# Gated cross-attention on one core: product and residual kept in the context's PSUM bank, memory loaded a step earlier, GpSimd's subtractions cut into pieces

## What is computed

```
memory_proj = memory @ W_mem.T                                # 375 x 512
attn  = softmax(x @ memory_proj.T / sqrt(512))
context = attn @ memory_proj
gate  = sigmoid(concat(x, context) @ W_gate.T + b_gate)
fused = x + gate * context
out   = fused * rsqrt(mean(fused^2) + 1e-6) * norm_w
```

## Time and profile before

| what | value |
|---|---|
| median of three runs | 345.56 us |
| profiled execution | 344.57 us |
| its span, first to last instruction | 342.8 us |
| mean granted TensorE clock | 0.935 |
| TensorE matmul busy | 295.7 us (86%) |
| VectorE busy | 210.1 us (61%) |
| ScalarE busy | 173.7 us (51%) |
| GpSimd busy | 173.3 us (51%) |

### The profile page before, as it was taken

One profiled execution on the slowest core, in us unless ns is written; L12 is line 12 of the kernel. 1 busy time (PEld: TensorE's weight loads), 2 busy tenths in 40 slices (PEclk: granted clock), 3 DMA queues, 4 the chain that ended last, 5 costly groups with the idle time before them and its releaser, 6 DMA issues. The chain is left out here.

```text
span 342.8 us, 4761 instructions
## 1 busy us (share of the span) xinstructions
PE 295.7 (86%) x1479; PEld 246.7 (72%) x1479; DVE 210.1 (61%) x356; ACT 173.7 (51%) x363; POOL 173.3 (51%) x135
## 2 busy tenths in 40 slices
PE   8998588899897799999897699999998599957791
PEld 5977477778786598788686598787687488846561
DVE  4994535856867526855876536757876635555644
ACT  5862535546636436454556446544655445425531
POOL 1342445834848544744857643745857732443502
PEclk9999699999999599999999589999999689998997
DMA  7957744867764573866855573775846563652421
GB/s 293 408 149 237 232 112 122 262 185 231 213 180 125 139 224 117 264 188 185 246 148 135 154 242 115 229 224 147 254 115 179 167 183 113 175 157 71 118 64 62
DMA packets 52872, 61.40 MB, mean 179 GB/s; under 512 B 38640, under 2 KB 38896, under 8 KB 52592
## 3 DMA queue, kind: packets, MB, share of 16 engines
q1 hardware_dynamic: 52848, 61.10, 59.4%
HBM read 43.25 MB, written 7.34 MB: 148 GB/s over the span
## 5 line engine op out<-in xcount | busy, mean ns | idle before, releaser
L886 POOL TENSOR_TENSOR memT_lo<-mems_raw,memT_hi 128x752 fp32r<-128x752 f32 x21 | 38.1, 1815 | 58.8 <-ACT memT_hi L540 58.8
L736 DVE STREAM_TRANSPOSE blocks_am<-am 128x256 f32<-128x256 f32 x32 | 14.2, 445 | 70.5 <-ACT am L588 70.5
L886 POOL TENSOR_TENSOR mem_lo<-mems_raw,mem_hi 128x768 fp32r<-128x768 f32 x22 | 48.1, 2188 | 10.6 <-ACT mem_hi L540 10.5
L904 POOL TENSOR_TENSOR guarded<-meansq,eps 128x1 f32<-128x1 f32 x27 | 5.5, 203 | 78.3 <-ACT work L597 78.2
L573 ACT ACTIVATE probs<-score_ps,shift 112x375 f32<-112x375 f32 x32 | 18.3, 573 | 46.8 <-DVE shift L716 46.8
L766 DVE SCALAR_TENSOR_TENSOR work<-work,rstd,norm_w 128x512 f32<-128x512 f32 (+1 forms) x29 | 38.6, 1334 | 1.1 <-POOL rstd L939 1.0
L602 ACT ACTIVATE work<-work 128x512 f32<-128x512 f32 (+1 forms) x29 | 17.8, 618 | 40.2 <-DVE work L745 40.2
L540 ACT ACTIVATE memT_hi<-mems_raw 128x752 fp32r<-128x752 f32 x22 | 18.3, 831 | 34.6 <-DMA mems_raw<-in_mems 34.5
L758 DVE SCALAR_TENSOR_TENSOR work<-work,x_rows 128x512 f32<-128x512 f32 (+1 forms) x29 | 34.4, 1189 | 0.3
L350 PE MATMUL gate_ps<-wgx_hi,xT_hi 128*128 128x512 f32 x108 | 33.2, 433 | 0.1
L352 PE MATMUL gate_ps<-wgx_lo,xT_hi 128*128 128x512 f32 x108 | 31.8, 419 | 0.0
(11 more groups left out here) (128 smaller groups left out, 719.0 us busy)
## 6 DMA issues: line engine op xcount, KB each, us to landing
mems_raw<-in_mems SPq DMA_DIRECT2D x20, 760.0 KB, 5.1
x_rows<-in_x SPq DMA_DIRECT2D x28, 256.0 KB, 5.3
out<-work SPq DMA_DIRECT2D x27, 256.0 KB, 5.5
first_raw<-in_mems SPq DMA_DIRECT2D x9, 760.0 KB, 4.8
pT_raw<-blocks_p SPq DMA_DIRECT2D x128, 48.0 KB, 2.6
xT_raw<-in_xT SPq DMA_DIRECT2D x7, 640.0 KB, 6.0
amT_raw<-blocks_am SPq DMA_DIRECT2D x128, 32.0 KB, 1.9
xT_raw<-in_xT SPq DMA_DIRECT2D x3, 512.0 KB, 6.0
```

The costliest lines, as they stand in the source:

```text
L736: dve.transpose(turned_am, am_blocks).then_inc(blocks_am_ready, 1)
L886: return pool.tensor_tensor(out, in_, high.bitcast(F32), ALU.subtract)
L904: pool.tensor_tensor(guarded[:, s], meansq[:, s], eps[:], ALU.add).then_inc(guarded_ready, 1)
```

## The change

- SyncE loads the memory of batch s+3 in step s where it loaded that of batch s+2; `load_mems(5)` is added to the opening. It now waits for the low parts of batch s itself, made in the same step.
- `gate_context` writes its product over the context in `ctx_ps`; `fuse` adds x there, in place; `square` (ScalarE) and `norm` (VectorE) read that bank. The SBUF tiles u and h go. `context(t)` therefore waits for `y_ready`, the norm of the tile before. The last tile's two halves use the two `q_ps` banks.
- ScalarE does `pT_high(s-1)` ahead of `exponentials(s)`, and `square` ahead of `amT_high`.
- VectorE does `norm(before)` ahead of `turn_am(s-1)` where it stood behind it.
- GpSimd's subtractions are one instruction per chunk: 2 for memT, 3 for mem, 4 for x.

```diff
-        work = sb("work", [P, 7, D])
-        z, h, y, u = work[:, 0:2], work[:, 2:4], work[:, 4:6], work[:, 6]
+        work = sb("work", [P, 6, D])
+        z, y = work[:, 0:2], work[:, 4:6]
...
-        late_ps = [ctx_ps, gate_ps[1]]
+        late_ps = q_ps
...
             load_mems(4)
+            load_mems(5)
...
-                if s + 2 < BATCHES:
-                    load_mems(s + 2)
+                if s + RAW < BATCHES:
+                    load_mems(s + RAW)
...
             def context(t, cols=ALL, bank=ctx_ps):
                 pe.wait_ge(wmT_lo_ready, EC)
-                if t > 0:
-                    pe.wait_ge(u_ready, t)
+                if bank is ctx_ps and t > 0:
+                    pe.wait_ge(y_ready, t)
...
-            def square(t, cols=ALL, i=0):
+            def square(t, cols=ALL, i=0, bank=ctx_ps):
...
-                act.activation(z[:, t % 2, cols], h[:, t % 2, cols], ACT.Square, scale=D ** -0.5,
+                act.activation(z[:, t % 2, cols], bank[:, cols], ACT.Square, scale=D ** -0.5,
...
+                if s - 1 < BATCHES:
+                    pT_high(s - 1)
                 for n in softmaxes_at(s)[:1]:
                     exponentials(n)
-                if s - 1 < BATCHES:
-                    pT_high(s - 1)
+                if before is not None:
+                    square(before)
                 if s - 2 < BATCHES:
                     amT_high(s - 2)
-                if before is not None:
-                    square(before)
...
-                dve.scalar_tensor_tensor(out=u[:, cols], in0=z[:, t % 2, cols], scalar=1.0, in1=bank[:, cols],
+                dve.scalar_tensor_tensor(out=bank[:, cols], in0=z[:, t % 2, cols], scalar=1.0, in1=bank[:, cols],
...
-                dve.scalar_tensor_tensor(out=h[:, t % 2, cols], in0=u[:, cols], scalar=0.5,
+                dve.scalar_tensor_tensor(out=bank[:, cols], in0=bank[:, cols], scalar=0.5,
                                          in1=x_rows[:, t % X_SLOTS, cols],
...
-                dve.scalar_tensor_tensor(out=y[:, t % 2, cols], in0=h[:, t % 2, cols],
+                dve.scalar_tensor_tensor(out=y[:, t % 2, cols], in0=bank[:, cols],
...
                     amT_low(s - 2)
+                if before is not None and before < LAST - 1:
+                    norm(before)
                 if s - 1 < BATCHES:
                     turn_am(s - 1)
                 for n in softmaxes_at(s)[1:]:
                     maximum(n)
-                if before is not None and before < LAST - 1:
-                    norm(before)
...
             def split_xT(g, unit):
                 c, n = UNITS[unit]
                 pool.wait_ge(xT_hi_ready, N_UNITS * g + unit + 1)
-                low(xT_lo[:, :, c:c + n], raw_of(unit), xT_hi[:, :, c:c + n]).then_inc(xT_lo_ready, 1)
+                for i in range(DC):
+                    piece = low(xT_lo[:, i, c:c + n], raw_of(unit)[:, i], xT_hi[:, i, c:c + n])
+                piece.then_inc(xT_lo_ready, 1)
...
-                low(memT_lo[:, n % 2], memT_raws[n % RAW], memT_hi[:, n % 2]).then_inc(memT_lo_ready, 1)
+                for c in range(EC):
+                    piece = low(memT_lo[:, n % 2, c], memT_raws[n % RAW][:, c], memT_hi[:, n % 2, c])
+                piece.then_inc(memT_lo_ready, 1)
...
-                low(mem_lo[:, n % 2], mem_raws[n % RAW], mem_hi[:, n % 2]).then_inc(mem_lo_ready, 1)
+                for c in range(KC):
+                    piece = low(mem_lo[:, n % 2, c], mem_raws[n % RAW][:, c], mem_hi[:, n % 2, c])
+                piece.then_inc(mem_lo_ready, 1)
```

More of the change, by code:

```diff
@@ L696, in _ @@
             for i, cols in enumerate(HALVES):
-                square(LAST, cols, i)
+                square(LAST, cols, i, late_ps[i])
         @block.vector
@@ L750, in gate_context, with fuse, norm @@
                 dve.wait_ge(ctx_done, t + 1 + i)
-                dve.scalar_tensor_tensor(out=u[:, cols], in0=z[:, t % 2, cols], scalar=1.0, in1=bank[:, cols],
+                dve.scalar_tensor_tensor(out=bank[:, cols], in0=z[:, t % 2, cols], scalar=1.0, in1=bank[:, cols],
                                          op0=ALU.add, op1=ALU.mult).then_inc(u_ready, 1)
-            def fuse(t, cols=ALL, i=0):
+            def fuse(t, cols=ALL, i=0, bank=ctx_ps):
                 dve.wait_ge(x_loaded[t % X_SLOTS], 16 * (t // X_SLOTS + 1))
                 dve.wait_ge(u_ready, t + 1 + i)
-                dve.scalar_tensor_tensor(out=h[:, t % 2, cols], in0=u[:, cols], scalar=0.5,
+                dve.scalar_tensor_tensor(out=bank[:, cols], in0=bank[:, cols], scalar=0.5,
                                          in1=x_rows[:, t % X_SLOTS, cols],
                                          op0=ALU.mult, op1=ALU.add).then_inc(h_ready, 1)
-            def norm(t, cols=ALL):
+            def norm(t, cols=ALL, bank=ctx_ps):
                 dve.wait_ge(rstd_ready, t + 1)
@@ L876, in _ @@
             for i, cols in enumerate(HALVES):
-                fuse(LAST, cols, i)
+                fuse(LAST, cols, i, late_ps[i])
             norm(LAST - 1)
-            for cols in HALVES:
-                norm(LAST, cols)
+            for i, cols in enumerate(HALVES):
+                norm(LAST, cols, late_ps[i])
         @block.gpsimd
```

## The result

| | before | after |
|---|---|---|
| median | 345.61 us (4 runs, 343.83 to 346.28) | 318.74 us (4 runs, 317.85 to 321.14) |
| ratio | 1 | 0.9241 [0.9178, 0.9304] |
| span of the profiled execution | 342.8 us | 316.4 us |
| mean granted clock | 0.935 | 0.956 |

The kernel became 26.9 us faster where 19.4 were forecast. The time lies within the range (317 to 337) but outside the band of the forecast itself (320 to 330), and the reasons don't all hold, as the experiments show.

The account below looks back on a forecast made before the run. The prediction took TensorE's own work plus its holes to bound the kernel. Terms -5.0 - 1.7 - 4.5 - 1.0 - 7.2 = -19.4 us from 344.57 gave 325.2, stated as 325.5; range 317 to 337 us.

Parts of the forecast that it names:

- The memory a step earlier: Memory load a step earlier: nearly all of ScalarE's 34.5 us DMA wait goes, but the term is only -1.7 us.
- Residual and norm in PSUM: VectorE's residual and norm take 0.69 us each, returning 34 us to VectorE; shorter TensorE waits for pT_low give -5.0 us.
- Steps 10, 18, 26: Steps without a tile: next score starts earlier, 1.5 us in each of three, -4.5 us.
- the clock: After the thin stretch in steps without a tile, the clock drops again but shorter: -1.0 us, bounds 0 and -7.
- the clock stays up: Rival: no clock drops at steps 10, 18, 26, giving 318 us; chance 0.08.
- Step 30: With the memory already there, score(30) to attend(30) takes 10.6 us instead of 16.5; whole term -7.2 us.
- Wrong if the exponential waits for pT: Sign against the forecast: ScalarE's exponential is held up by pT; no size given.
- The hole only changes its name: Rival: only the DMA wait goes, everything else is bounded elsewhere, such as late pT; gain 11 us, 334 us; chance 0.12.
- Context's wait for the norm: Context now waits for the previous tile's norm; 0.8 us of slack in the shortest steps, priced at 0.
- GpSimd's pieces: 122 extra GpSimd pieces at 0.15 us, 18 us, hidden except where counted.
- SyncE's wait for mem_lo: SyncE waits for mem_lo(s) before loading; GpSimd ends it about when SyncE used to reach that load, priced at nothing.

Follow-up runs that it names:

- a2: Changed kernel with product and residual in SBUF tiles again, orders kept, context waiting for `u_ready`: 321.01 us, 0.9374 of the kernel before.
- b2: Kernel before with the PSUM part alone, the norm still behind `turn_am`: 344.12 us, 1.0032 of the kernel before.
- b3: Kernel before with the earlier load of the memory alone: 319.26 us, 0.9306 of the kernel before.
- b1: Changed kernel with ScalarE's old order, exponential ahead of `pT_high` and `amT_high` ahead of `square`: 317.35 us, 0.9241 of the kernel before.
- a1: Changed kernel with the memory load back at its old place (batch s+2): 344.69 us, 1.0059 of the kernel before.
- a3: Changed kernel with each GpSimd subtraction as one instruction again: 319.45 us, 0.9303 of the kernel before.
- d1: Kernel before with the last of `move_am`'s four transfers cut in two, same bytes: 359.4 us, 1.0425 of the kernel before.

## Why the prediction was right in its time and wrong in its reasons

**The step that failed is "The memory a step earlier", -1.7 us**, and under it the opening reading that the kernel "is bound by TensorE's own work plus its holes". I saw ScalarE's 34.5 us and what is queued behind (`attended` among it), but followed that queue only to TensorE's next wait, not round through `turn_am` and SyncE's list back to the load itself. Had I laid two loads side by side in the timeline (68.50 and 78.04) and asked what stands between them, the 9.5 us would have shown. Alone this edit is worth 23.9 us. So the time lies within the range by luck in part: a term of 1.7 stood for 23.9, and terms that are worth little beside it filled the sum.

**Residual and norm in PSUM, -5.0.** The durations came as said, 0.69 and 0.75 us, the two groups gave 32.4 of the 34 us back, and the ordinary steps' waits for pT_low fell from 6.0 to 1.0 us (0.63 and 0.41). PSUM isn't needed for that last point: in a2, with SBUF tiles and pieces, no ordinary step waits for pT_low. And a hole inside a step that waits for its ring is no gain: alone the edit gives +1.0 us (b2, the interval holds 1). In the changed kernel it is worth about 2.1 (a2). Of the ordinary steps' -14.0 us the earlier load alone gives 12.6 (b3); 8.1 had been summed from holes (5.0 + 1.7, and the 1.4 ahead of step 30).

**Steps 10, 18, 26, -4.5, and the clock, -1.0.** Together -8.2 was measured. The score began 5.3 us after the end of the one before, not 6. The step as it became (start us, us, engine, line, what, count, idle before):

```profile
103.46 0.82 ACT L541 ACTIVATE memT_hi<-first_raw 128x752 fp32r<-128x752 f32 x1
...
103.79 0.60 PE L358 MATMUL am_bank<-mem_hi,wgc_hi 128*112 128x256 f32 x3 [1.74 <-DVE wgc_hi L704]
...
104.45 1.91 POOL L887 TENSOR_TENSOR memT_lo<-first_raw,memT_hi 128x376 fp32r<-128x376 f32 x2
...
106.62 0.57 PE L351 MATMUL score_ps<-memT_hi,qT_hi 128*112 128x376 f32 x2 [2.23 <-POOL memT_lo L887]
...
107.83 1.91 PE L351 MATMUL gate_ps<-wgx_hi,xT_hi 128*128 128x512 f32 x4
```

Against the earlier trace rows, the chain exponential, square, memT_hi, memT_lo is the one followed, with fewer gaps; the two pieces take 1.91 against 1.77, the 0.15 as priced. The clock drops again, as predicted: four gate matmuls at 107.83 take 1.91 us, 1.2 GHz. What came otherwise is how long it stays low. Granted clock of two of the three stretches (us, TensorE busy and count, and so on, granted clock, DMA share, GB/s):

```profile
107.00:110.40 3.40, 3.40 (x13) 2.82 (x12) 1.60 (x5) 1.91 (x5) 1.44 (x3) 0.58 0.41 64
175.00:182.00 7.00, 4.46 (x14) 3.83 (x15) 2.60 (x6) 3.58 (x9) 4.89 (x7) 0.56 0.57 166
```

By the granted clock's course the low stretches last 3.4, 6.8 and 3.4 us where before had 10.2 each time. Their parts within steps 11, 19 and 27 add up to 11.3 us, before to 16.9, and a busy TensorE loses half of such a stretch: an estimate of 2.8 us for the 2.6 that these steps gained. The rival "the clock stays up", at 318 us, did not happen, though its time is the nearest; it also counts 1.0 of the clock twice, which is in the 325.5 already, so that its own terms give 319.5.

**Step 30, -7.2.** From score(30) to the attend of batch 30 I worked out 10.6 us, where before had 16.5. Measured: 278.75 to 289.29, 10.5. That chain was right, and the 1.4 us in front went too. What I missed lies behind it: from that attend to the end before takes 23.8 us and after 27.1. Four rows of the tail, timeline of the changed kernel:

```profile
289.29 0.58 PE L351 MATMUL am_bank<-mem_hi,wgc_hi 128*112 128x256 f32 x3 [1.69 <-POOL mem_lo L887]
...
303.86 0.60 ACT L598 ACTIVATE work<-ctx_ps 128x512 f32<-128x512 f32 x1 [1.57 <-DVE ctx_ps L759]
...
304.44 0.41 ACT L541 ACTIVATE amT_hi<-amT_raw 128x256 fp32r<-128x256 f32 x1
304.99 0.73 PE L351 MATMUL gate_ps<-wga_hi,amT_hi 128*128 128x512 f32 x2 [2.78 <-ACT amT_hi L541]
```

The last amT landed at 302.16, but `amT_high` stands behind `square` by the new order, and the square waits for the residual; TensorE idles 2.78 us (0.51 before at this place, 1.6 in b1). From the attend of batch 31 to these matmuls it takes 10.6 us (294.40 to 304.99), 8.0 before (324.27 to 332.30). The other 0.9 us lie behind 304.99, where the clock is at half from 305.5 to 308.9. With ScalarE's old order the time from score(31) to the end is that of before (b1: 30.10), so the 2.7 us that the tail lost are the swap's. The term paid 2.7 of its 5.8 beyond the part in front. I had priced the swap of `square` and `amT_high` at 0.2 here and at nothing elsewhere.

**The swap of `pT_high` and the exponential.** "Wrong if the exponential waits for pT": it does, since `pT_high` stands in front of it and waits for pT 12 times, 17.5 us, and steps 6, 14 and 22 became 9.95, 9.25 and 9.74 us, where b1 has 9.07. It is the rival "the hole only changes its name", true in mechanism at three steps and in the tail, at 2 us or less in all by the times (b1) and not at the 9 that it was given. This is also why the whole change is no faster than the load alone: what the PSUM part wins in steps 5, 13 and 21 (3.1 us against a2) the swap loses in 6, 14, 22 and the tail.

**Costs priced at nothing.** Context's wait for the norm: right in the changed kernel, no such wait. b2 shows that the cover was the norm's place ahead of `turn_am`: behind it, 17 waits, 13.6 us; ahead of it, with the ring still closed (a1), none. The Trainium skill, Perfetto Trace Analysis, "Matmuls", asks that groups rotate through PSUM banks; here one bank held to the norm costs nothing with the norm early and 13.6 us of TensorE's waiting with it late, so it is the holder's release that decides. GpSimd's pieces: 17.0 us more busy time, 18 predicted, hidden in this kernel (a3). SyncE's wait for mem_lo: it now sets the load's issue (72.50 right behind 72.43), and no `memT_hi` waited for it outside the start, so nothing was lost by it that the traces show.

**The size.** 26.9 against 19.4 by the medians, 26.4 against 19.4 by the traces. The ordinary steps give 5.9 us more than summed, steps 10, 18, 26 with their followers 2.7 more, the opening 1.5 that I hadn't counted; step 30 with the tail 3.1 less. (From the median of 345.56 the sum gives 326.2; the 325.5 stated lies between that and the 325.2 from the profiled execution.)

## What to carry to other kernels

When one engine waits again and again for a load, put two successive issues of that load side by side and follow back from the second: if the chain reaches the first, it is a ring, the mean distance between them is the floor of the mean step, and holes elsewhere within the step may be worth nothing until it is cut, as VectorE's were here (b2). Look at the issuing queue above all: a load that depends on nothing new, standing behind a transfer that waits for computed data, inherits that transfer's chain. A small dose in the suspected ring tells it from a guess: 0.66 us added to each of some 27 turns came back as 14.7 us, and as 4.5 with the ring open.

## What was not expected of the hardware

- An issue of a transfer on SyncE takes 0.33 to 0.60 us of its queue in most rows of before, with single ones up to 1.64 (349 of 367 are at 0.65 or less), and its bytes hardly matter: four of `move_am` take 2.48 us in the median, and five 3.14 when one of them is cut in half (d1), where a load of a batch's whole memory often takes 0.54.
- GpSimd's one-element instruction L912 takes 438 ns on average, 203 before, on the same data. GpSimd comes to it earlier now, while VectorE's subtraction with two SBUF operands (L704) has only just begun: at 103.33 it takes 0.45 us beside L704 at 103.20. All 24 instances beside an L704 take 0.45 to 0.53 us, the 3 without one 0.19. The block between the two engines thus acts both ways, as the Trainium skill, SBUF — State Buffer, "Who interferes with whom", has it for such pairs; there was no run that took VectorE's part away, so the cause is read, not shown.
